# First layer of a graph network on one core: every sixth supertile gathers all five tiles with GpSimd

## The reference

```
h = jnp.maximum(_layernorm(x, axis=-1), 0.0)
x = x + segment_sum(h[src] * edge_weight[:, None], dst)        # first layer
h = jnp.maximum(_layernorm(x, axis=-1), 0.0)
x = x + _L1_gnn_ref(h, edge_index, edge_attr_4, edge_attr_32, W1, b1, W2, b2, si_w0, si_w1)
```

## Time and profile before

| | us |
|---|---|
| median of three runs | 9360.98 |
| lowest and highest of them | 9352.47, 9393.81 |
| profiled execution, its own time | 9461.48 |
| its span | 9459.5 |
| stage of the first layer's loop in it | 89.5 to 4010 |

### The profile page before, as it was taken

How to read it: one execution, slowest core, us unless ns; L and a number is a source line. 1 busy time by engine, 2 the same in 40 slices (tenths; PEclk the granted TensorE clock), 3 DMA queues, 4 the chain that set the end, 5 groups by cost and what they waited for, 6 DMA issues and landing times.

```text
span 9459.5 us, 174094 instructions
## 1 busy us (share of the span) xinstructions
PE 7449.8 (79%) x50435; PEld 3591.8 (38%) x50435; DVE 4950.2 (52%) x11385; ACT 3090.8 (33%) x13342; POOL 5058.3 (53%) x5374
## 2 busy tenths in 40 slices
PE   5877877888778887768887878777788888777787
PEld 2333333333333333333333333333333333333333
DVE  4444444444444444455555555555555555555555
ACT  1222222222222222233444444444434444444444
POOL 5656666666655666544544554554445545455543
PEclk9999999999999999878888888888888888888888
DMA  2111111111111111011111111111111111111111
GB/s 71 21 21 20 21 21 21 20 21 21 20 21 20 21 21 21 17 34 22 24 23 23 24 23 23 24 23 23 23 23 24 23 23 23 24 24 23 24 23 23
DMA packets 352525, 224.60 MB, mean 24 GB/s; under 512 B 114265, under 2 KB 349353, under 8 KB 351864
## 3 DMA queue, kind: packets, MB, share of 16 engines
q0 software_dynamic: 170080, 87.42, 6.6%
q1 hardware_dynamic: 182418, 136.86, 5.4%
HBM read 218.75 MB, written 5.12 MB: 24 GB/s over the span
## 4 chain that ended last, share of the span: by engine, by line
PE 33%; another core or an unknown queue 28%; issue 16%; DVE 14%; DVEq 4%; ACT 3%; DMA 0%; ACTq 0%; POOL 0%; SPq 0%; POOLq 0%
PE w_ps L641 19%; PE hp_ps L769 4%; PE w_ps L722 4%; DVEq L939 3%; DVE prod L1099 3%; PE w_ps L726 2%; PE w_ps L651 2%; DVE squares L1117 2%; DVE t L1104 1%; DVE prod L966 1%; PE sc_ps L738 1%; ACT coef L554 1%; ACT near L597 1%; DVE onehot L934 1%
## 5 line engine op out<-in xcount | busy, mean ns | idle before, releaser
L417 POOL DMA_INDIRECT z<-h_table,idx x5315 | 5026.2, 946 | 4265.9 <-DVE prod L1108 1838.5
L641 PE MATMUL w_ps<-stage,prod 128*128 128x448 bf16 x13125 | 2882.5, 371 | 837.1 <-issue 671.0
L641 PEld LDWEIGHTS w_ps<-stage,prod 128*128 128x128 bf16 x13125 | 1274.6, 101 | 2200.7 <-issue 1203.8
L496 ACT ACTIVATE z<-z,squares 128x32 f32<-128x32 f32 x3125 | 790.5, 309 | 3109.3 <-issue 2231.2
L769 PE MATMUL hp_ps<-stage,squares 128*128 128x448 bf16 x6510 | 1501.2, 380 | 57.2 <-issue 34.4
L946 DVE TENSOR_TENSOR acc<-acc,w_ps 32x32 f32 x1250 | 213.4, 171 | 2088.6 <-remote 1847.1
L547 ACT ACTIVATE hid<-w_ps,b_sb 128x320 f32<-128x320 f32 x625 | 329.3, 527 | 2364.0 <-remote 1452.5
L769 PEld LDWEIGHTS hp_ps<-stage,squares 128*128 128x128 bf16 x6510 | 622.5, 104 | 954.1 <-issue 533.9
L722 PE MATMUL w_ps<-w_sb,hid 64*128 64x256 f32 x5000 | 861.2, 471 | 0.0
L738 PE MATMUL sc_ps<-prod,onehot 128*32 128x344 f32 x5000 | 667.2, 479 | 178.3 <-issue 134.1
L1088 DVE TENSOR_TENSOR p<-w_ps,scalars 128x320 f32<-128x320 f32 x625 | 303.7, 486 | 861.6 <-remote 822.3
(11 more groups left out here) (97 smaller groups left out, 5942.5 us busy)
## 6 DMA issues: line engine op xcount, KB each, us to landing
z<-h_table,idx POOLq DMA_INDIRECT x5315
feat<-key_table SPq DMA_DIRECT2D x311, 192.0 KB
ft_sh_sb<-in_ft_sh SPq DMA_DIRECT2D x625, 90.0 KB
h_table<-big SPq DMA_DIRECT2D x10, 312.5 KB
x_sb<-in_x SPq DMA_DIRECT2D x1, 1562.5 KB
prod<-in_dst_flat SPq DMA_DIRECT2D x1, 1562.5 KB
rel_sb<-in_dst_t SPq DMA_DIRECT2D x1, 1562.5 KB, 36.4
out<-x_sb SPq DMA_DIRECT2D x5, 312.5 KB
```

The costliest lines, as they stand in the source:

```text
L417: pool.indirect_dma_start(z[:, r, u, :], None, rows, bass.IndirectOffsetOnAxis(ap=idx[:, r, u:u + 1], axis=0)).then_inc(z_in[r], 16)
L496: last = nc.scalar.activation(z[:, r, u, :], z[:, r, u, :], ACT.Copy, scale=ew_all[:, bass.ds(n * G + u, 1)])
L641: mm = pe.matmul(fold_ps[:, k, 0:NC * D], pick[k][:, blk, :], parts[:, t, :, blk, :], start=(blk == 0 and t == 0), stop=(blk == GB - 1 and ...
```

## The change

In the first layer the last supertile of each turn of six (r = 5) gathers all five tiles with GpSimd, where `on_pe0(r)` is false. It has no keys to compare, no pick matmuls and no selection. The other five are done as before. The semaphores of the picks count one for each supertile that picks, by `nth0(b, r)`, and no longer n; `slot_before(b, r)` names the pick that used the same one of the three buffers last. Counts that were n in the waits are changed to these.

```
+    def on_pe0(r):
+        return r < R0 - 1
+    def nth0(b, r):
+        return b * (R0 - 1) + r
+    def slot_before(b, r):
+        return nth0(b, r - PEG) if r >= PEG else nth0(b - 1, r + PEG if r + PEG < R0 - 1 else r)
...
-                    sp.wait_ge(pick_ready, n - R0 + BATCH)
+                    sp.wait_ge(pick_ready, nth0(b - 1, r) + (BATCH if on_pe0(r + BATCH - 1) else BATCH - 1))
...
-            supertiles(pool, R0, gathers(R0, h0_dram, idx0_ready, z0_in, sum0_ready, lambda r, s: GT))
+            supertiles(pool, R0, gathers(R0, h0_dram, idx0_ready, z0_in, sum0_ready, lambda r, s: GT if on_pe0(r) else G))
...
-                act.wait_ge(z0_in[r], (b + 1) * 16 * GT)
+                act.wait_ge(z0_in[r], (b + 1) * 16 * (GT if on_pe0(r) else G))
...
-                    if u == GT:
-                        act.wait_ge(selected, n + 1)
+                    if u == GT and on_pe0(r):
+                        act.wait_ge(selected, nth0(b, r) + 1)
...
-                if s is None or s < S:
-                    pe.wait_ge(pick_ready, n + 1)
+                if on_pe0(r) and (s is None or s < S):
+                    pe.wait_ge(pick_ready, nth0(b, r) + 1)
                     if s is None or s >= PEG:
-                        pe.wait_ge(selected, n - PEG + 1)
+                        pe.wait_ge(selected, slot_before(b, r) + 1)
...
-                    dve.wait_ge(picked, n - PEG + 1)
+                    dve.wait_ge(picked, slot_before(b, r) + 1)
...
-                if s is None or s < S:
+                if on_pe0(r) and (s is None or s < S):
                     make_pick(n, b, r, s)
...
-                    select_group(n - 3, bv, v)
+                    if on_pe0(v):
+                        select_group(n - 3, bv, v)
```

More of the change, by code:

```diff
@@ L960, in select_group @@
                 k = r % PEG
-                done = n * 2
+                m = nth0(b, r)
+                done = m * 2
                 nc.vector.tensor_tensor(group_hot[:], iota_ps[:, 0:NC], group_of[:, bass.ds(n, 1)].to_broadcast([P, NC]),
                                         ALU.is_equal).then_inc(group_step, 1)
-                dve.wait_ge(picked, n + 1)
+                dve.wait_ge(picked, m + 1)
                 dve.wait_ge(group_step, done + 1)
```

## The result

The changed kernel takes 9527.0 us, the median of 4 runs (9514.03 to 9533.63). The kernel before took 9377.4 us beside it. The ratio is 1.0161, with a 95% interval of 1.0141 to 1.0181: slower by 150 us.

What follows compares the result with a forecast made beforehand. GpSimd's gathers, holding TensorE's signals, were taken to set the first layer's pace. +155 us for the fifth gathers and -5 for fewer bursts of four gave +150, scaled +148 on 9361: 9510 us, range 9380 to 9620.

Steps and rivals of the forecast that it cites:

- GpSimd sets the pace, because its gathers hold TensorE's signals: First layer's loop: signals wait until a burst is over, so GpSimd's wall time is the stage's, 1.565 us a gather; 63%.
- cause or companion: First layer: whether bursts of gathers cause TensorE's late signals or only go along with them; the prediction said cause.
- three readings for the cause: Waits grow with the burst; TensorE runs gapless at 165 ns a matmul while GpSimd idles; the second layer shows the same.
- The fifth gather, 1.49 us: Every sixth supertile, first layer: 1.25 us step plus 0.25 us longer wait, 104 times, +155 us (bounds +130 and +163).
- The explanation behind the 0.25 us: GpSimd's wait grows 0.25 us a gather, 1.73 after four to 2.72 after eight; signals come 2.1 us after the last.
- The rule of constant cost: A skill page's fixed cost near 2.0 us for a GpSimd DMA: the wait would stay constant, total about 9490.
- The picks at 0, with -5 for fewer bursts of four: Work taken from TensorE and VectorE costed at 0; fewer bursts of four worth -5 us, between -40 and 0.
- The order around the supertile without a pick at 0: Two sums back to back may idle TensorE up to 2.3 us more a turn, hidden in its free time: 0.
- The rival that priced the hole at 239 us: TensorE's 2.3 us hole behind the supertile without a pick adds to the gather: +239, 9750 us; chance 8%.
- Longer bursts: Rival, first layer: bursts of 12 or 13 replace three of 8, saving 0.5 us a turn: 9460 us; chance 12%.
- The signs to look for: Profile after: 5419 gathers, stage of 4070 us, waits of 2.7 us or more, about 1.56 us a gather, TensorE about 67%.
- The sign against my reading: The reading is wrong if GpSimd's waits at a turn's start last longer than those behind its other bursts.

Runs made afterwards that it cites:

- e8: The kernel before, with the first layer's gathers replaced by SyncE's plain loads of fixed rows of the same size, all picks kept: 8378.19 us beside 9374.
- e1: The kernel before, with a fifth gather into an unread spare tile in every sixth supertile, all picks kept: 9523.87 us, ratio 1.0155.
- e9: The changed kernel without its fifth gather, that tile a constant and the sixth supertile's pick still left out: 9378.62 us, ratio 1.0011 to the kernel before.
- e11: The kernel before, with each first-layer gather fetching 64 rows in place of 128, same number of gathers: 9430.76 us beside 9404.16.
- e0: The kernel before, unchanged, run once more for a second profile: 9371.09 us, ratio 1.0002.
- e7: The changed kernel once more, on a third chip, against the kernel before there: 9511.68 us, ratio 1.0158.
- e3: The kernel before, with a spare gather in every second supertile, 312 gathers more, all picks kept: 9752.94 us, ratio 1.0419.
- e2b: The same kernel as e9, run on the faster chip beside a kernel before of 6858: 6858.86 us, ratio 1.0001.
- e5: The same kernel as e8, run on the faster chip beside a kernel before of 6858: 6578.27 us, ratio 0.9593.

## Why the prediction was right

It said 9510 us, +148 on the median; the kernel takes 9527.0, +150. A part of that closeness is luck: the gather was priced 5 us too high in all (155 against 150, below), and the 5 us taken off for bursts of four rested on one execution. The two cancel. Step by step:

**GpSimd sets the pace, because its gathers hold TensorE's signals.** Right that the gathers hold them and that their number sets the pace. e8 removes the gathers and the hold is gone; e1 adds a gather and nothing else and loses 1.55%; e9 takes 104 picks and wins nothing. Of what the prediction called doubtful (cause or companion) e8 is the proof. It is not GpSimd's own time that counts, though: in e11 eight gathers take 0.35 us less and the stage gains nothing. One of the prediction's three readings for the cause was weaker than it looked. The 165 ns a matmul at the loop's start are of a stretch in which 104 of 124 matmuls are those of picks, against 3363 of 4963 in the steady one; the pace to set beside 201 ns is that of e8, 1000 us for 6876 matmuls, 145 ns.

**The fifth gather, 1.49 us.** Right in kind, slightly too high. The rows of all traces together give the length of a burst with its wait, from start to start, between 300 and 3900 us:

| gathers in the burst | us, median | kernels |
|---|---|---|
| 4 | 6.3 to 6.4 | e0, e7, e11 |
| 8 | 12.2 | e0, changed, e1, e7, e9, e11 |
| 9 | 13.6 | changed, e1, e3, e7 |
| 12 | 17.9 | changed, e7 |
| 13 | 19.4 | changed, e7 |

From eight to thirteen that is (19.4 - 12.2) / 5 = 1.44 us a gather. 104 x 1.44 = 150, which is what the first layer lost against e0. The totals give 1.50 us a gather for e1, 1.32 for e7 and 1.23 for e3, so 1.44 is a middle value and not a constant to three digits. The prediction had 0.25 us of growth in the wait, from the four and the eight of the first profile (2.72 for eight); the median waits in e0 are 1.64 and 2.53, so (2.53 - 1.64) / 4 = 0.22.

**The explanation behind the 0.25 us.** This part fell. I had the signals come free 2.1 us after the burst's last gather. e11 shows that the time is not hung on the gathers' end: when they end earlier, the signals do not come earlier. Nor does it follow TensorE's work, since bursts of eight take 12.2 us with a pick missing (e9) and without. It follows the count: about 1.44 us a gather and some 0.7 us a burst (12.2 - 8 x 1.44). The numbers of the prediction survive because, with gathers of 128 rows, both pictures give the same sum.

**The rule of constant cost.** The Trainium skill, "DMA: Bandwidth & Descriptors", section "Anatomy of one DMA — SWDGE (gpsimd) path", gives a DMA from GpSimd a fixed cost near 2.0 us, by which the prediction had a total of about 9490. For the DMA itself the traces agree: a gather's last completion packet ends 2.07 us after its start in e0 and 2.06 in e2b, and within a burst this doesn't grow. The prediction set this cost against GpSimd's wait, and there it was wrong to say that the trace doesn't agree: the wait ends with TensorE's signal and is another thing. It does grow, 1.7 us behind four gathers, 2.5 behind eight, 2.65 behind nine and 3.5 behind thirteen, and that growth the sum needed. On the faster chip no wait is to be seen at all, and there the fifth gather should cost its step alone: 104 x 1.249 = +130 us, 6988 us. That is an estimate; the changed kernel was not run there.

**The picks at 0, with -5 for fewer bursts of four.** The 0 was right (e9: 1.0011, with 0 inside the interval; e1 and the change differ by 0.0006). The -5 rested on 54 bursts too many, a count that goes with the execution and not with the kernel: e0 has 8 bursts of four in all, the changed kernel 16. It was harmless, and so was the long first profile as a whole, since the sum was a difference.

**The order around the supertile without a pick at 0.** Right. The hole is there, larger than the 2.3 us I gave it (6.20 us in the timeline, of which 2.9 are held time and 3.2 VectorE's), and the clock falls from 0.94 to 0.86. But e9 has both (7.24 us idle before a pick at 2034.23, clock 0.87) and loses nothing. The rival that priced the hole at 239 us is out.

**Longer bursts.** They came, but rarely: 14 of thirteen and 7 of twelve among 286 between 300 and 3900 us. At some 0.7 us saved for each burst that two become one, 21 of them are 15 us at most. So this rival was a part of the truth, and small. Its three and a third waits a turn were too few for its own rows: 342 in 2301 / 24 = 96 turns are 3.6.

**The signs to look for.** 5419 gathers, as said. Stage of 4070 us: from the loop's first pick the changed kernel took 3974 us, since the first profile was 80 us longer than the next one; the difference of 150 is the one that holds. Waits of 2.7 us and more: 2.5 to 2.65 by median. 1.56 us a gather: 1.53, which is also what e0 has (3500 / 2283). TensorE at 67% of the stage: 71% of the loop, since the picks that are left take longer at the lower clock. The sign against my reading, longer waits at a turn's start, is there by 0.15 us: 2.65 us by median behind the bursts of nine that end a turn, 2.5 behind the others. But the bursts of nine of e3, which leaves out no pick, have 2.64 as well.

## What to carry to other kernels

Before shifting work from one engine to another, find out which engine's instructions carry the time, and not which is busiest: here TensorE was busiest with 79%, and taking 4.1 us of it and 2.4 us of VectorE in every turn was worth nothing, while each gather given to GpSimd cost 1.2 to 1.5 us. Split such a change into its halves and run them apart, as e1 and e9 do. A second profile of the unchanged kernel is cheap, and tells which features of the first are the kernel's and which are one execution's.

## What was not expected of the hardware

The same kernel takes 9368 us on one chip and 6858 on another. The whole difference is in the stages with indirect gathers (first layer 3824 us in e0; 3117 in e2b, which costs the same as the kernel before on its chip; second layer 5345 and 3530), and none is in the stage without them (2824.3 and 2823.8). What sets the two kinds apart no row says; each chip was used once and only one was fast, so that it is the chip itself is not shown either.

Where TensorE is held, a burst of n gathers with its wait takes about 0.7 + 1.44 n us, whether a gather fetches 64 rows or 128. A guess that fits is that something that every gather does in the same number is worked off at that pace and stands in front of TensorE's signals. Its data are not that, since their packets keep the pace of 1.25 us. Nor are its 16 counts on the semaphore by themselves: the loads of e8 make as many each, 886 loads in 1000 us on the slower kind of chip where e0 has 652 gathers, and TensorE runs through them. What it is stays open.

No version here beats both kernels. e5 and e8 show what would: rows brought in without GpSimd's gathers would take 1000 us off the first layer on the slower kind of chip and some 290 on the faster one. But they read fixed rows, and no way to fetch the right ones without an indirect gather was tried.
